# One table of steps for a round: pairs of heads on the row halves, feed-forward behind its own attention, the next batch's projections inside it

## What is computed

```
x = x + 0.5 * FFN(LN(x))       # "call 0": two layers
x = x + ATTN(LN(x))            # global attention, 16 heads of 16 features
x = x + 0.5 * FFN(LN(x))       # "call 1": the same two layers
```

```
h = shift_token(x)                       # second half of the features comes from the token before
q, k, v = split(h @ wqkv)                # 8 heads of 64
q, k = rotary(l2norm(q) * qs), rotary(l2norm(k) * ksc)
o = local attention, windows of 128 tokens, each query block sees its own and the preceding key block
x = x + o @ wo
h = LN(shift_token(x)) * lg + lb
a, g = split(h @ w1 + b1)                # 682 features each
x = x + (a * gelu(g)) @ w2 + b2
```

## Time and profile before

| what | value |
|---|---|
| median of 3 runs | 4402.12 us |
| profiled execution, its own time | 4415.59 us |
| its span, first to last instruction | 4413.9 us |
| PE busy | 4113.5 us (93%) |
| PEld busy | 3533.3 us (80%) |
| DVE busy | 2840.4 us (64%) |
| ACT busy | 2313.8 us (52%) |
| POOL busy | 2175.8 us (49%) |
| granted TensorE clock, mean | 0.961 |

### The profile page before, as it was taken

The page is one execution under the profiler, slowest core; times in us unless marked ns, Lnnn a source line. Parts: engine busy times, 40 slices in busy tenths (PEclk is TensorE's granted clock), DMA queues, the critical chain, the costliest instruction groups (busy, mean ns, idle before and its releaser), DMA issues.

```text
span 4413.9 us, 76198 instructions
## 1 busy us (share of the span) xinstructions
PE 4113.5 (93%) x24064; PEld 3533.3 (80%) x24064; DVE 2840.4 (64%) x7678; ACT 2313.8 (52%) x5456; POOL 2175.8 (49%) x2179
## 2 busy tenths in 40 slices
PE   5799999999999879999999999888999999999998
PEld 3688888778788768888888888766878888788887
DVE  6567777767777546655565565556766677676774
ACT  2455566555655435444454454444565555565554
POOL 3345544445444435655555565534544455444552
PEclk8799999999999989999999999977999999999999
DMA  3000001010000010000000000000000010100000
GB/s 123 14 13 15 18 13 37 19 38 23 23 23 19 15 48 15 15 15 7 11 15 16 1 15 30 15 29 10 18 13 18 13 40 17 42 22 18 25 16 24
DMA packets 101364, 99.87 MB, mean 23 GB/s; under 512 B 11708, under 2 KB 98376, under 8 KB 100936
## 3 DMA queue, kind: packets, MB, share of 16 engines
q1 hardware_dynamic: 100936, 94.66, 6.7%
HBM read 56.91 MB, written 29.36 MB: 20 GB/s over the span
## 4 chain that ended last, share of the span: by engine, by line
PE 66%; POOL 10%; issue 10%; DVE 9%; DMA 2%; ACT 2%; POOLq 0%; SPq 0%; DVEq 0%; ACTq 0%
PE psum L1308 16%; PE psum L1309 15%; PE psum L1310 15%; PE psum L1490 10%; PE psum L1472 4%; POOL rinv L594 3%; PE psum L1567 2%; POOL turned_qk L589 2%; DMA nrm<-xmid 1%; POOL ge_lo L649 1%; DVE turned_qk L1034 1%; PE psum L1547 1%; POOL probs L626 1%; POOL pT_lo L606 1%; POOL turned_qk L584 1%
## 5 line engine op out<-in xcount | busy, mean ns | idle before, releaser
L649 POOL TENSOR_TENSOR ge_lo<-ge,ge_hi 128x512 fp32r<-128x512 f32 x512 | 722.4, 1414 | 521.1 <-DVE ge_hi L1227 272.9
L626 POOL TENSOR_SCALAR probs<-probs,rz 128x256 f32<-128x256 f32 (+1 forms) x1024 | 443.2, 451 | 702.0 <-DVE rz L1117 702.0
L870 ACT ACTIVATE ge<-psum 128x512 f32<-128x512 f32 x512 | 306.5, 599 | 605.7 <-PE psum L1567 595.9
L812 ACT ACTIVATE probs<-probs,nb,rq 128x256 f32<-128x256 f32 (+1 forms) x1024 | 576.2, 570 | 72.9 <-DVE nb L1149 70.8
L1227 DVE CAST ge_hi<-ge 128x512 fp32r<-128x512 f32 x512 | 250.3, 490 | 524.7 <-ACT ge L870 523.3
L1490 PE MATMUL psum<-kT,qT 64*128 64x256 f32 (+1 forms) x2048 | 500.7, 393 | 4.6 <-DVE mx L1142 3.2
L594 POOL TENSOR_TENSOR rinv<-ssq,minus_half 128x16 f32<-128x16 f32 x128 | 374.1, 2923 | 204.4 <-DVE ssq L1027 198.2
L1124 DVE TENSOR_TENSOR pT_lo<-psum,pT_hi 128x512 fp32r<-128x512 f32 (+1 forms) x512 | 295.8, 619 | 264.4 <-ACT pT_hi L797 262.1
L1142 DVE CUSTOM_DVE_ANT_0 probs<-psum,mask 128x256 f32<-128x256 f32 (+1 forms) x1024 | 344.7, 386 | 155.9 <-PE psum L1490 155.7
L1490 PEld LDWEIGHTS psum<-kT,qT 64*128 64x128 f32 x2048 | 352.3, 204 | 90.2 <-issue 38.6
L742 ACT ACTIVATE probs<-psum 128x512 f32<-128x512 f32 x256 | 153.3, 599 | 505.3 <-DVE turned_sin L1011 505.1
(11 more groups left out here) (182 smaller groups left out, 12009.4 us busy)
## 6 DMA issues: line engine op xcount, KB each, us to landing
xnext<-stream SPq DMA_DIRECT2D x32, 512.0 KB, 3.9
stream<-xmid SPq DMA_DIRECT2D x16, 512.0 KB, 3.1
nrm<-xmid SPq DMA_DIRECT2D x32, 254.0 KB
x_all<-L_attn_x SPq DMA_DIRECT2D x8, 512.0 KB, 7.3
stream<-x_all SPq DMA_DIRECT2D x8, 512.0 KB, 3.9
nrm<-L_attn_x SPq DMA_DIRECT2D x8, 512.0 KB, 3.9
x_mid<-xmid SPq DMA_DIRECT2D x8, 512.0 KB, 2.9
gx<-x_mid SPq DMA_DIRECT2D x8, 512.0 KB, 4.2
```

The costliest lines, as they stand in the source:

```text
L626: last = nc.gpsimd.tensor_scalar(probs[:, h % 3, i, a:], probs[:, h % 3, i, a:], rz[:, h, i:i + 1], 1.0, ALU.mult, ALU.mult)
L649: nc.gpsimd.tensor_tensor(ges[1][:, k % 4, :], ge[:, k % 4, :], f32(ges[0][:, k % 4, :]), ALU.subtract).then_inc(S["g_lo"], 1)
L812: last = nc.scalar.activation(probs[:, s % 3, i, a:], probs[:, s % 3, i, a:], ACT.Exp, bias=nb[:, s, i:i + 1], scale=rq[:, 0, i, s:s + 1], ...
L870: nc.scalar.activation(ge[:, k % 4, :], RB[k % 2], ACT.Exp, scale=GSCALE, accum_out=gz[:, h, t:t + 1]).then_inc(S["g_exp"], 1)
```

## The change

Each engine gets one table of steps for a round, and `steps` reads it. A token with "-" belongs to batch n-1, with "+" to batch n+1, without a sign to batch n.

- A unit of attention is now a pair of heads and half of the query blocks, eight units as before eight heads (`unit`). S makes a unit's four score products so that the head in rows 0 to 63 and the head in rows 64 to 127 alternate. T, H, L and A follow for the same unit; A multiplies by key block, in pieces of one or two query blocks.
- The output product W, the residual addition x, the shift, the normalisation (l, r, s, j, n, nh, nl) and the first part of the feed-forward (g0 a0 g1 a1 g2) are of batch n in round n. The rest of the feed-forward of batch n runs in round n+1 among its heads.
- The projections of batch n+1 run in round n: z, q0 k0 k1 q1 k2 q2 v0 and some turns among the heads and output products, the rest after W3.
- There is one xmid tile. SP loads the residual into it a second time (`x_residual`), after the store of the batch before; the copy xin is gone.
- ACT's squares wait for PE's projection and not for DVE's rotary products; they have a buffer of their own. The feed-forward's hidden halves have their own tiles hid_hi and hid_lo, and hid_r one apart from gate.
- Weights use two staging buffers wbuf0 and wbuf1; the parts of a load are spread over steps i0 i1 i2 and f0 f1 f2.
- PE derives its waits for a free bank from the table (`bank_before`).
- Each round issues two more Gelu and exp changes on ACT (G2 G3, E0, G4, E3, G5).
- The scratch of dynamic DMAs is set to 1024.

```diff
+UNITS = HEADS
+PE_STEPS = ("S0 -g3 -w0 S1 -w1 -a2 S2 T0 -a3 +z0 -g4 +z1 -a4 S3 T1 A0 S4 A1 T2 S5 -w2 S6 T3 -w3 A2 S7 T4 A3 +q0 "
+            "T5 +k0 -g5 +k1 A4 T6 -w4 +q1 +Q0 A5 A6 -w5 T7 +k2 +q2 W0 A7 +K0 W1 +v0 W2 W3 B +Q1 +v1 +v2 +K1 +q3 "
+            "+k3 +K2 n0 n1 +v3 +Q2 g0 a0 g1 +Q3 a1 +K3 g2").split()
+ACT_STEPS = ("-G2 -G3 E0 E1 i0 -u2 H0 E2 i2 +zh0 +zh1 -G4 -u3 H1 E3 i1 O0 H2 E4 E5 H3 E6 -u4 H4 O1 E7 +sq0 H5 +sk0 "
+            "-G5 +sk1 H6 -u5 +sq1 +Qc0 H7 +sk2 +sq2 O2 f0 O3 f1 +Kc0 +vh0 +Qc1 +vh1 +vh2 +sq3 +Kc1 +sk3 +Kc2 nh0 "
+            "nh1 +vh3 G0 f2 +Qc2 G1 +Qc3 u0 +Kc3 u1").split()
+DVE_STEPS = ("X0 X1 R0 -y2 X2 i0 R1 -y3 L0 +zl0 +zl1 -y4 R2 X3 i2 L1 X4 i1 R3 X5 L2 R4 P0 X6 L3 R5 X7 L4 P1 R6 "
+            "+rq0 L5 +ss0 R7 +rk0 -y5 L6 +rq1 +c0 +rk1 +ss1 -F -e L7 +ss2 +rq2 +rk2 P2 f0 P3 f1 +c1 +vl0 +c2 x l "
+            "+vl1 r +vl2 +rq3 j +ss3 nl0 nl1 B +rk3 y0 f2 +vl3 +c3 y1 +Y").split()
+POOL_STEPS = ("-ul1 N0 -ul2 N1 N2 N3 -ul3 N4 N5 N6 +b0 -ul4 +p0 +d0 -ul5 N7 +b1 +p1 +d1 +p2 +d2 +b2 s +b3 +p3 +d3 "
+            "ul0").split()
+def unit(u):
+    pair, half = u // 2, u % 2
+    return (2 * pair, 2 * pair + 1), (2 * half, 2 * half + 1)
...
     def rounds(...)
+        first(n0)
+        a_round(n0, prev=False, load=2 * call)
+        a_round(n0 + 1)
+        with eng.Fori(0, B - 3) as j:
+            a_round(n0 + 2 + j)
+        a_round(n0 + B - 1, switch=2 * call + 1)
+        a_round(n0 + B, load=2 * call + 1)
+        with eng.Fori(0, B - 2) as j:
+            a_round(n0 + B + 1 + j, final=B * (call + 1))
+        a_round(n0 + ROUNDS - 1, nxt=False, final=B * (call + 1))
+        last(n0 + ROUNDS - 1, B * (call + 1))
...
     SP
+        def x_residual(m):
+            need_apart(sp, (S["x_stored"], 16 * m))
+            sp.dma_start(xmid[:], tokens(stream, m)).then_inc(S["xmid_in"], 16)
-            need(sp, S["dve_y"], m)
+            need(sp, S["dve_old"], m)
             sp.dma_start(nrm[1:P, :, P:D], xmid[0:P - 1, :, P:D]).then_inc(S["shift_in"], 16)
             sp.dma_start(nrm[0:1, 1:NT, P:D], xmid[P - 1:P, 0:NT - 1, P:D]).then_inc(S["shift_in"], 16)
+            def a_round(n, prev=True, nxt=True, load=None, switch=None, final=0, call=call):
+                if prev and final:
+                    x_old(n - 1, call)
+                if switch is not None:
+                    w_qkv(switch)
+                if load is not None and load % LAYERS:
+                    w_o(load)
                 if nxt:
+                    x_ahead(n + 1, ...)
+                if prev:
+                    keep(n - 1, final, call)
+                x_residual(n)
                 if load is not None:
                     w_f(load)
+                shift(n)
...
     DVE
+                if kind == "x":
+                    dve.wait_ge(S["pe_wo"], PAIRS * (m + 1))
+                    dve.wait_ge(S["xmid_in"], 16 * (m + 1))
+                    for b in range(2):
+                        xv = xmid[:, 2 * b:2 * b + 2, :].rearrange("p t d -> p (t d)")
+                        V.tensor_tensor(xv, ACC[b], xv, ALU.add).then_inc(S["dve_wo"], 1)
+                if kind == "r":
+                    dve.wait_ge(S["shift_in"], 32 * (m + 1))
+                    dve.wait_ge(S["dve_st"], 2 * m + 1)
+                    for t in range(NT):
+                        last = V.bn_stats(st[:, t, 1, :], nrm[:, t, P:D])
...
     PE
+                if kind == "S":
+                    heads, blocks = unit(i)
+                    for b, t in enumerate(blocks):
+                        a = P if t == 0 else 0
+                        for side in range(2):
+                            rows = slice(side * DH, (side + 1) * DH)
+                            last = mm(RB[side][:, b * 2 * P + a:(b + 1) * 2 * P], qT[rows, i // 2, t * P:(t + 1) * P],
+                                      kT[rows, i // 2, (t - 1) * P + a:(t + 1) * P], start=True, stop=True)
+                            if b == 1:
+                                last.then_inc(S["pe_s"], 1)
+                if kind == "A":
+                    for side in range(2):
+                        for j in sorted({j for j, _ in cols}):
+                            at = [k for k, (j_, _) in enumerate(cols) if j_ == j]
+                            t = cols[at[0]][1]
+                            last = three(PAIR[p % 2][:, t * P:(t + len(at)) * P],
+                                         [v[:, j, p, side * DH:side * DH + P] for v in v_s],
+                                         [x_[:, i % 2, side, at[0] * P:(at[-1] + 1) * P] for x_ in pT], ...)
...
-    nc = bacc.Bacc("TRN2", target_bir_lowering=False, num_devices=1)
+    nc = bacc.Bacc("TRN2", target_bir_lowering=False, num_devices=1, dynamic_dma_scratch_size=1024)
```

More of the change, by code:

```diff
@@ L170, in build @@
     m2 = [turned_sin[:, w, :] for w in range(2)]
+    squares = sb("squares", [P, 2, INNER], c=ffn_mem)
+    sq = [squares[:, w, :] for w in range(2)]
     qT = sb("qT", [P, PAIRS, N], c=ffn_mem)
@@ L257, in build, with rounds @@
     block = ctx.enter_context(nc.Block())
[L259 to L272, removed]
+    def rounds(eng, call, start, a_round, first, last):
         n0 = call * ROUNDS
         start(2 * call)
[L280 to L306, removed]
-        one(n0 + ROUNDS - 2, 0, ROUNDS - 2)
-        a_round(n0 + ROUNDS - 1, n0 + ROUNDS - 3, n0 + ROUNDS - 2, 1, ahead=False, f_final=True, g_final=plain, nxt=None)
-        last_f(n0 + ROUNDS - 1)
+        first(n0)
[9 more added lines that the diff above has]
+        last(n0 + ROUNDS - 1, B * (call + 1))
     W_A, W_F = 3, 3
@@ L357, in sequences, with g_steps @@
         body(B - 1, 1, "last")
-    def steps(which, tail):
+    def g_steps(which, tail):
         return range(G_STEPS + (tail if which == "last" else 0))
@@ L563, in _ @@
         stage_end(pool, 0)
-        def prep(n, stored):
-            pass
         def start(stage):
@@ L642, in sequence @@
                 def sequence(b, r, which):
-                    for k in steps(which, TAIL):
+                    for k in g_steps(which, TAIL):
                         if k < G_STEPS:
@@ new lines, in some_steps @@
+                if kind == "w":
+                    if fresh_w2 is not None and m == n:
+                        weights_done(pe, w_base(fresh_w2) + W_A + W_F)
+                        fresh_w2 = None
+                    pe.wait_ge(S["pool_u"], (FJ + 1) * m + i + 1)
+                    for t in range(NT):
+                        last = three(ACC[t // 2][:, (t % 2) * D:(t % 2 + 1) * D],
+                                     [u[:, i % 2, t * P:(t + 1) * P] for u in hid],
+                                     [w_[:, i, :] for w_ in w2_s],
+                                     i == 0 and t % 2 == 0, i == FJ, skip_group_check=True)
+                    last.then_inc(S["pe_w2"], 1)
@@ L1538, in last_f, with a_round, last @@
+            def a_round(n, prev=True, nxt=True, load=None, switch=None, final=0, call=call):
+                left = some_steps(n, prev, nxt, call, None, load, switch)
+                if load is not None:
+                    weights_done(pe, w_base(load) + W_A + W_F)
+            def last(m, final, call=call):
+                some_steps(m + 1, True, False, call, -1)
                 stage_end(pe, 1 + 2 * call)
-            rounds(pe, call, prep, early, a_round, start, w_a, last_f)
+            rounds(pe, call, start, a_round, first, last)
```

1059 lines of the change are left out of this document (475 added, 584 removed).

## The result

The changed kernel takes 4733.01 us (4 runs, 4731.79 to 4735.12) against 4404.78 us for the kernel before on the same chip (4395.25 to 4408.54): a ratio of 1.0749, 95% interval 1.0731 to 1.0768. It is slower by 7.5%. The forecast was 4695 us with a range of 4550 to 4860; the sign and the mechanism hold, and the size is 38 us short.

A forecast was written before the change was run, and what follows sets the result against it. PE was taken as full (84.8 of 88.7 us a round). Rounds of 82.1 + 17.0 + 2.3 = 101.4 us, with weight changes, ends, fill and drain, add 147 us per stage, 294 for both: 4695 us, range 4550 to 4860.

The forecast's parts named there:

- The chain from x to n0: Same-batch steps x, shift, r, vl2, rq3, j between last output product and transposes n0: 23.7 us, shift 15.8 of it.
- PE's hole: Between W3 and n0, PE has 6.7 us of work during the 23.7 us chain, so idles 17.0 us each round.
- The cold clock, 2.3 us a round: After PE's idle stretch the clock is at 1.2 GHz when dense matmul follows: half of 4.6 us, 2.3 us added.
- Score pairs: Two heads' scores on adjacent row halves overlap partly: 2.2 us a pair instead of 3.42, 4.9 us less per round.
- the rival of full overlap: Score products on the two row halves overlap fully, ratio exactly two: 4640 us in all, chance 0.07.
- Attention times values: Same columns in narrower pieces: 3.25 us a pair instead of 2.7, 2.2 us more per round.
- PE's work in a round: PE's busy work per round of one batch and layer: 84.8 - 4.9 + 2.2 = 82.1 us.
- Other stalls at nothing: PE's waits elsewhere in the round put at nothing against 3.9 us before; up to 4 us could come back.
- The period: Length of a steady round: 82.1 + 17.0 + 2.3 = 101.4 us against 88.7.
- Rounds that change weights: The two rounds of a stage that change weights add about 8 us, as ACT's f0 waits for its chunk.
- Fill and drain: Start and end of each stage give back about 10 us: half a feed-forward left at the end, not two.
- the shift is not 15.8 us: Rival: shifted half lands like a 3.9 us write, hole 5 us, no clock loss, 4270 us; faster outcomes together 0.09.

The follow-up runs named there:

- Experiment 1: Shift of 127 partitions split into DMAs of 112 and 15: on the changed kernel 4358.68 us, on the kernel before 4381.23 us.
- experiment 3: Changed kernel, shift not split, plus 13.6 us of filler matmuls a round between q3 and k3: 4754.73 us.
- experiment 2: Changed kernel with split shift: vl2 and rq3 ahead of r 4432.08 us; only vl2 ahead 4364.68 us; that plus filler matmuls before n0 4325.47 us.
- experiment 4: Changed kernel with a unit's score products head by head: 4736.67 us; with all from rows 0 to 63: 4856.13 us; also 64 products added once in four orders.
- the one-half version: Changed kernel with every score product taken from rows 0 to 63: 4856.13 us.
- The round with filler: Changed kernel with split shift, vl2 ahead of r and three groups of six useless matmuls between K2 and n0: 4325.47 us.

## Why the prediction was right, and where its terms were off

The likeliest case came true: a hole per round made by the shift, now that the feed-forward follows its own attention. The steps, each against its measurement:

- **The chain from x to n0.** Predicted 23.7 us, measured 24.0. Landing 16.1 us where 15.8 was taken. The 15.8 came from the start of r; the remark beside it, that L467 sits 11.3 us behind L466, misreads: it begins 0.8 us behind and its issue lasts 11.3 us. Experiment 1 shows it by removal (-374 us), experiment 3 by filling it (435 us of work for 22).
- **PE's hole.** Predicted 17.0 us, measured 14.8 + 0.5. The other 1.7 us are not idle: k3 and K2 ran at 1.2 GHz inside the hole (the window 574 to 586 has the clock at 0.50), so the 6.7 us of work took longer. The idle time of a whole round is 17.0 us all the same ((201.00 - 166.96) / 2), but by luck: 15.3 in the hole and 1.6 in waits that I had put at nothing.
- **The cold clock, 2.3 us a round.** Mis-sized, and in this kernel wrongly placed. I put it behind n0. In the round shown the clock was back before n0 began, so none of it lay on the path; over five steady rounds n0 to Q2 takes 2.3, 2.9, 2.3, 3.1 and 2.3 us, which makes 0.3 us a round. The same effect is real where the waits are short: 1.3 us a round in experiment 2, 0.7 in experiment 3. My 2.3 came from a tail where the clock was at 0.50 when dense work began after its wait; here k3 and K2 ran at 0.50 ahead of n0, in time that was idle anyway.
- **Score pairs.** Predicted 2.2 us a pair by in-order issue, measured 1.98. The picture behind the number was wrong: by it, the order by head should have cost 3 us a round, and it cost nothing (experiment 4). In alternation the ratio is 1.92, close to the rival of full overlap; a unit of eight instructions shows less of it, 1.92 / 1.06 = 1.81; why was not tested. The Trainium skill, "TensorEngine Tiling (Array Packing)", Theoretical Speedup, says up to 2x for 64 rows; the trace agrees with 1.92 for a long run. The gain on the path is 3.5 us a round and not 4.9, by the one-half version.
- **Attention times values.** Predicted 3.25 us a pair; the half units take 1.3 and 2.1 us (539.94 to 541.27, 531.19 to 533.28), 3.4 together.
- **PE's work in a round.** Predicted 82.1 us. The round with filler and a clock of 1.00 throughout has 85.4 us busy, of which 4.1 are filler: 81.3.
- **Other stalls at nothing.** Of the 3.9 us of before, 1.6 us remain as named waits in the round from 565 to 665. The forecast had left up to 4 us open here.
- **The period.** Predicted 101.4 us, measured 100.6. That it is so close is partly luck, since the errors have both signs: the cold clock 2.0 and PE's work 0.8 us too much, the other stalls 1.6 too little.
- **Rounds that change weights.** Predicted 8 us in all, measured 117 us for the round 869 to 986 alone, 16 over a steady one, and about 3 and 2 for its neighbours: 21 us. In that round PE waits 5.3 us for oT_lo, 1.8 for pT_lo and 1.6 for hT_lo, none over 0.6 in a steady one. The term could have been read from the kernel before: its three rounds there take 95.0, 102.6 and 91.8 us (781.52 to 1070.87), 23 over three steady ones, and PE waits 5.4 us for oT_lo there too. What makes oT_lo late was not tested.
- **Fill and drain.** Predicted 10 us given back per call. The first shift is issued 7.3 us later (160.88 against 153.54), the end behind the last one is 5.8 us shorter, so 1.5 us are lost in the first call. In the second 3.8 us are lost, 10.0 ahead of the first shift less 6.2 behind the last. The round that has no projections is 9.5 us shorter than a steady one, as predicted.

For the first call that is 15 x (100.6 - 101.4) = -12 us, +13 for the weights, +11.5 for fill and drain, some 13 us more than forecast. The second comes to 157.4 us, 10 more than the 147 forecast: 24 in all, and 318 between the spans instead of 294. The rest of the 38 us is that the sum was made against a profiled execution 13 us above its median, while the one after lies at its median.

Of the rivals, "the shift is not 15.8 us" named the right point of decision. With a landing of 3.7 us the same order of work runs at 4358.68 us, faster than before; I had put it at 4270. Of the 88 us between, 51 are the steady rounds, 88.9 us against 87.2: from 603.45 to 692.40 PE is idle 5.5 us, near the 5.1 of that sum, but busy 83.5 where the work at the full clock is 81.3. That is the clock, which I had called "without loss of clock". Some 28 us are the rounds that change weights, mis-sized here as above, and the rest is about the 13 us between the profiled execution and its median. So the change was a good one standing behind a bad transfer: with the shift split in both, it is 22.6 us ahead of the old order, and with vl2 moved and filler 56 us.

## What to carry to other kernels

Before you move a step, follow the latencies that lie next to it, not its busy time: a transfer of 16 us cost nothing in the rounds where another phase lay beside it, 24.8 us in 4400 over the whole kernel, and 374 us when its own consumer came next. Then ask why that transfer is long, since its shape was the cheapest thing to change here. And when work is moved into a wait, look at what it had covered where it stood: both filler moves of real work (rq3, v3) opened a wait of about the same size elsewhere. And when the clock falls in a wait, ask whether its slow stretch ends inside the hole or behind it.

## What the runs showed of the hardware

- A DMA of 127 partitions landed 16.1 us after its data was ready, with the 16 DMA engines busy to a share of 0.07; the same bytes as 112 + 15 partitions landed in 3.7 us.
- Products of 64 rows on the two halves ran 1.92 times as fast as on one when they alternated and 1.87 times in twos; with eight on one half and then eight on the other the ratio was 7.17 / 6.42 = 1.12.
- With a wait of 2.4 us in each round, the granted clock fell from 1.00 to 0.50 just behind the end of that wait, at 521.5 us in one round and at 610.3 in the next, for 3.4 and 6.8 us; only the second stretch reached the work behind the next wait, and that round took 1.4 us longer. Useless matmuls in a wait of 4.4 us kept it at 1.00 and made the kernel 39 us faster. More such matmuls in the hole of 14.8 us moved the cold stretch from where it was free to where it was not, and made it 22 us slower.
